# Scores of a head pair: two stacked 128-row products per head, or three 64-row products per head on the two halves of the array

## The reference

```python
qh = (q @ w_q).reshape(B, L, 16, 64).transpose(0, 2, 1, 3)
kh = (k @ w_k).reshape(B, L, 16, 64).transpose(0, 2, 1, 3)
vh = (v @ w_v).reshape(B, L, 16, 64).transpose(0, 2, 1, 3)
attn = einsum('bhqd,bhkd->bhqk', qh / 8, kh) + add_attn
attn = where(mask == 0, -1e9, attn);  attn = softmax(attn)
out = einsum('bhqk,bhkd->bhqd', attn, vh) @ w_o + residual;  out = layernorm(out)
```

## Time and profile before

| | |
|---|---|
| median of 3 runs | 3976.67 us (3975.65 to 3981.02) |
| the profiled execution | 3981.92 us |
| its span, first to last instruction | 3980.1 us |
| granted TensorE clock, mean | 0.99 |
| busy: PE, DVE, ACT, POOL | 95%, 68%, 56%, 46% |
| stages L0a and L0b | about the first 1440 us |

### The profile page before, as it was taken

The page is one execution under the profiler, slowest core; times in us unless marked ns, Lnnn a source line. Parts: engine busy times, 40 slices in busy tenths (PEclk is TensorE's granted clock), DMA queues, the critical chain, the costliest instruction groups (busy, mean ns, idle before and its releaser), DMA issues.

```text
span 3980.1 us, 63494 instructions
## 1 busy us (share of the span) xinstructions
PE 3767.7 (95%) x20700; PEld 2799.8 (70%) x20700; DVE 2724.9 (68%) x5801; ACT 2233.9 (56%) x4852; POOL 1847.6 (46%) x1905
## 2 busy tenths in 40 slices
PE   8999999999999998999999998999999979999999
PEld 6777677767777765666666766666666658888887
DVE  6666666677777777888888777888888853333334
ACT  6555555555555556777877767777777741111111
POOL 4444344344334345767767665666767631001001
PEclk9999999999999999999999999999999989999999
DMA  6666676554545466676666447776666671111000
GB/s 199 196 201 192 183 209 181 139 149 132 138 127 131 129 189 169 172 178 170 167 167 165 136 133 190 190 186 186 171 176 168 165 233 56 38 38 53 32 32 32
DMA packets 842517, 586.72 MB, mean 147 GB/s; under 512 B 611792, under 2 KB 660944, under 8 KB 841168
## 3 DMA queue, kind: packets, MB, share of 16 engines
q1 hardware_dynamic: 824400, 532.33, 50.0%
q10 hardware_dynamic: 17792, 50.33, 3.6%
HBM read 197.68 MB, written 238.55 MB: 110 GB/s over the span
## 4 chain that ended last, share of the span: by engine, by line
PE 40%; ACT 6%; DVE 6%; issue 5%; POOL 3%; DMA 3%; SPq 1%; DVEq 0%; POOLq 0%; ACTq 0%
PE psV L1529 5%; PE psT L1498 4%; PE psS L1477 3%; PE psJ L1422 3%; PE psS L1422 3%; PE psS L1424 3%; PE psS L1423 3%; PE psJ L1423 3%; PE psJ L1424 3%; POOL QS L2346 3%; PE psT L1422 2%; PE psT L1424 2%; PE psT L1423 2%; ACT PR L1805 2%; DVE PR L2001 1%
## 5 line engine op out<-in xcount | busy, mean ns | idle before, releaser
L2346 POOL TENSOR_SCALAR QS<-QK 32x1024 fp32r<-32x1024 f32 (+2 forms) x1152 | 1228.3, 1066 | 893.3 <-DVE QK L2015 434.9
L1805 ACT ACTIVATE PR<-PR,MN 128x512 f32<-128x512 f32 x1536 | 1101.5, 718 | 674.9 <-DVE MN L1997 518.1
L1997 DVE CUSTOM_DVE_ANT_0 PR<-psS,RAW 128x512 f32<-128x512 f32 x1024 | 694.2, 682 | 429.7 <-PE psS L1474 313.8
L1498 PE MATMUL psT<-ID,PR 128*128 128x128 f32 x3912 | 599.5, 276 | 95.8 <-ACT PR L1805 94.9
L1498 PEld LDWEIGHTS psT<-ID,PR 128*128 128x128 f32 x3912 | 475.8, 141 | 231.4 <-ACT PR L1805 142.3
L1529 PE MATMUL psV<-plain 128*32 128x512 f32 (+1 forms) x3072 | 510.3, 612 | 34.9 <-DMA plain<-split_rows 21.8
L1477 PE MATMUL psS<-QS 128*128 128x512 f32 x1024 | 456.8, 448 | 26.1 <-DVE PR L2001 14.0
L2001 DVE TENSOR_SCALAR_CACHE_REDUCE PR<-psS 128x512 f32<-128x512 f32 x512 | 345.3, 682 | 122.4 <-PE psS L1477 119.5
L1844 ACT ACTIVATE PR<-psS,COLS 128x512 f32<-128x512 f32 x128 | 88.3, 690 | 547.0 <-PE psS L1424 542.3
L2093 DVE COPY plain<-psT 128x512 f32<-128x512 f32 x530 | 361.2, 681 | 0.2 <-PE psT L1498 0.2
L2067 DVE CAST QK<-PR 128x512 fp32r<-128x512 f32 x128 | 59.2, 463 | 398.0 <-ACT PR L1844 352.6
(11 more groups left out here) (142 smaller groups left out, 8343.5 us busy)
## 6 DMA issues: line engine op xcount, KB each, us to landing
split_rows<-plain SPq DMA_DIRECT2D x366, 256.0 KB, 2.7
split_rows<-RAW SPq DMA_DIRECT2D x192, 256.0 KB, 2.5
x<-Y SPq DMA_DIRECT2D x96, 256.0 KB, 2.4
RAW<-x SPq DMA_DIRECT2D x96, 256.0 KB, 3.6
W<-kept ACTq DMA_DIRECT2D x12, 2048.0 KB, 11.3
Y<-x SPq DMA_DIRECT2D x96, 256.0 KB, 3.4
kept_c<-R SPq DMA_DIRECT2D x32, 512.0 KB, 3.9
kept<-ROWS SPq DMA_DIRECT2D x32, 512.0 KB, 3.6
```

Of the source, the lines that this page charges most:

```text
L1498: mm = nc.tensor.transpose(dst[:, kt * P:(kt + 1) * P], prob(st, k)[:, kt * P:(kt + 1) * P], ID[:, :])
L1805: nc.scalar.activation(prob(st, k), prob(st, k), ACT.Exp, bias=MN[:, k % 8:k % 8 + 1], scale=-1.0, accum_out=row_sums(st, SM, g)[:, qt, j: ...
L1997: nc.vector.tensor_tensor_reduce(out=prob(st, k), in0=psS[:, n % 2], in1=FB[:, k % NT], scale=-st.scale, scalar=BIG, op0=ALU.add, op1=ALU. ...
L2346: nc.gpsimd.tensor_scalar(to, pair, 1.0, 1.0, ALU.mult, ALU.mult).then_inc(stacked, 1)
```

## The change

In L0a and L0b the stacked copy goes. `score_pair` computes the same query tile of both heads of a group together: three matmuls for each head, with the 64 rows of that head as contraction, in turn for the first and second head, into the two banks of `psS`. The three are Q high by K high, Q high by K low and Q low by K high. Score tiles are numbered so that an even and the next odd one are the two heads of a group (`part`); the even step issues all six matmuls and the odd one none. The pair waits until both banks have been evacuated. `MAX` of the odd tile stands 0.75 slot before its old place, just behind that of the even one, and its `EXP` 0.25 slot earlier. POOL has no `STACK` step in these stages. `QS`, free now, takes Q and K of the odd groups, so that `J_HI` waits for scores of two groups earlier and no longer for the stacking. The stages of width 32 keep stacking.

```diff
 WIDE = {
-    "TILE": (1, 2, 3, 4),
-    "SENT": (1, 1.5, 2.5, 3.5),
+    "MAX": (0, -0.75),
+    "TILE": ((1, 0.75), (2, 2), (3, 3), (4, 4)),
+    "SENT": ((1, 1), (1.5, 1.5), (2.5, 2.5), (3.5, 3.5)),
...
-    "STACK": ((-1.5, -1, -1), (-5, -5, -5)),
...
+def part(st, k):
+    if st.dk == 32:
+        return divmod(k, NT)
+    group, n = divmod(k, 2 * NT)
+    return 2 * group + n % 2, n // 2
...
-        def qk(st, g):
-            return FB.bitcast(F32R) if bank(st, g) else QK
+        def qk(st, g, n):
+            if laid(st) and g % 2:
+                return QS[:, 1, n] if n < 3 else QS[:, 0, 2]
+            return QK[:, n]
...
+            def score_pair(st, k, b):
+                n = tal["s"].next()
+                if k % 2:
+                    return
+                g, qt = k // (2 * NT), part(st, k)[1]
...
+                pe.wait_ge(s_evac, tal["s"].done(n - 1))
+                tile = slice(qt * P, (qt + 1) * P)
+                for q, kk in ((0, 2), (0, 3), (1, 2)):
+                    for j in range(2):
+                        rows = slice(j * st.dk, (j + 1) * st.dk)
+                        mm = nc.tensor.matmul(psS[:, (n + j) % 2], qk(st, g, q)[rows, tile], qk(st, g, kk)[rows],
+                                              start=(q, kk) == (0, 2), stop=(q, kk) == (1, 2))
+                        if (q, kk) == (1, 2):
+                            mm.then_inc(s_full, 1)
...
-                if st.dk == 64:
-                    nc.tensor.matmul(psS[:, n % 2], q[:, tile], kk, start=True, stop=False)
-                    mm = nc.tensor.matmul(psS[:, n % 2], q[:, tile], k_lo, start=False, stop=True)
```

More of the change, by code:

```diff
@@ L227 @@
 SECOND = {
-    "TILE": (1, 2, 3, 4),
-    "SENT": (1, 2, 3, 5.6),
+    "MAX": (0, 0),
+    "TILE": ((1, 1), (2, 2), (3, 3), (4, 4)),
+    "SENT": ((1, 1), (2, 2), (3, 3), (5.6, 5.6)),
     "PV": (8, 8.5, 10, 10),
@@ L384, in timetable @@
         add(s, "SCORE", s)
-        add(s, "MAX", s)
+        add(s + table["MAX"][s % 2], "MAX", s)
         names = ("EXP", "SPLIT", "BOUNCE", "FETCH") if s in sent(st, b) else ("EXP", "TURN", "P_HI", "P_LO")
         for step, after in zip(names, table["SENT" if s in sent(st, b) else "TILE"]):
-            add(s + after, step, s)
+            add(s + after[s % 2], step, s)
     for h in range(NH):
@@ L398, in timetable @@
                 add(NT * h + (after[g] if isinstance(after, tuple) else after), step, g)
-        for piece in range(3):
+        for piece in range(3 if st.dk == 32 else 0):
             add(NT * h + table["STACK"][0 if h % st.per_group == 0 else 1][piece], "STACK", (h, piece))
@@ L1087, in count_turns @@
                 b = batch + off if at is None else at
-                if step == "EXP":
+                if step == "SCORE":
+                    score_at[st.name, b, k] = len(score_at) + 1
+                elif step == "EXP":
                     exp_at[st.name, b, k] = len(exp_at) + 1
@@ L1312, in fetch @@
                 sp.wait_ge(bounced[n % 4], times(n))
-                if last_product(st, b, k // NT):
-                    sp.wait_ge(pv_full, last_product(st, b, k // NT))
-                sp.dma_start_transpose(probs_of(ring(st, b, k // NT), k % NT).bitcast(U16),
+                h, qt = part(st, k)
+                if last_product(st, b, h):
+                    sp.wait_ge(pv_full, last_product(st, b, h))
+                sp.dma_start_transpose(probs_of(ring(st, b, h), qt).bitcast(U16),
                                        split_rows[n % 4].rearrange("q h k -> (q h) k")).then_inc(fetched[n % 4], 16)
@@ L1327, in run @@
                         if st.bias:
-                            tal["s"].mark(("side", k % NT))
+                            tal["s"].mark(("side", part(st, k)[1]))
                         if st.dk == 64:
@@ L1457, in x_turn @@
                 mm.then_inc(j_full, 1)
+            def score_pair(st, k, b):
[3 more added lines that the diff above has]
+                g, qt = k // (2 * NT), part(st, k)[1]
+                if qt == 0:
+                    split = max(tal["j"].marked(((kind, g), st.name, b)) for kind in "QK")
+                    pe.wait_ge(j_evac, tal["j"].done(split))
+                pe.wait_ge(s_evac, tal["s"].done(n - 1))
[7 more added lines that the diff above has]
+                            mm.then_inc(s_full, 1)
             def score(st, k, first):
@@ L1464, in score @@
                     if first and st.name == "SA" and h < 2:
-                        pe.wait_ge(qs_zero, 2 + h)
+                        pe.wait_ge(qs_zero, 1 + h)
                     i = tal["stack"].next()
@@ L1469, in score @@
                 tile = slice(qt * P, (qt + 1) * P)
-                q, kk, k_lo = (QS[:, h % 2, c] for c in range(3))
-                if st.dk == 64:
-                    nc.tensor.matmul(psS[:, n % 2], q[:, tile], kk, start=True, stop=False)
-                    mm = nc.tensor.matmul(psS[:, n % 2], q[:, tile], k_lo, start=False, stop=True)
-                else:
-                    mm = nc.tensor.matmul(psS[:, n % 2], q[:, tile], kk, start=True, stop=True)
-                mm.then_inc(s_full, 1)
+                q, kk = (QS[:, h % 2, c] for c in range(2))
+                nc.tensor.matmul(psS[:, n % 2], q[:, tile], kk, start=True, stop=True).then_inc(s_full, 1)
             held, gathered = {}, {}
@@ L1492, in turn @@
                 dst = turn_place(st, b, k)
-                at, head = ring(st, b, k // NT), (st.name, b, k // NT)
+                h = part(st, k)[0]
+                at, head = ring(st, b, h), (st.name, b, h)
                 if held.get(("head", at)) != head:
@@ L1631, in run @@
                     first = b == 0
-                    if step == "SCORE":
+                    if step == "SCORE" and laid(st):
+                        score_pair(st, k, b)
+                    elif step == "SCORE":
                         score(st, k, first)
@@ L1765, in context_hi, with projection_hi @@
                 nc.scalar.activation(cT[:, 0, kt], loaded("cs", buffer), ACT.Copy).then_inc(cs_hi, 1)
-            def projection_hi(st, name):
+            def projection_hi(st, name, b):
                 n = tal["j"].next()
@@ L1770, in projection_hi @@
                 kind, g = name[0], name[1]
-                if kind in "QK":
-                    used = tal["stack"].marked(("group", bank(st, g)))
+                if kind == "V":
+                    return
+                if laid(st):
+                    i, before = STAGES.index(st) * B + b, g - 2
+                    if before < 0:
+                        i, before = i - 1, before + NG
+                    if i >= 0:
+                        act.wait_ge(s_evac, 2 + score_at[STAGES[i // B].name, i % B, 2 * NT * (before + 1) - 1])
+                else:
+                    if st.name == "SA" and b == 0 and g == 0:
+                        act.wait_ge(s_evac, 2 + score_at["L0b", B - 1, 2 * NT * (NG - 1) - 1])
+                    used = tal["stack"].marked("group")
                     if used is not None:
                         act.wait_ge(stacked, tal["stack"].done(used))
[L1775 to L1778, removed]
                 act.wait_ge(j_full, tal["j"].done(n))
                 col = bias_col(st, kind, g)
-                nc.scalar.activation(qk(st, g)[:, 2 * "QK".index(kind)], psJ[:, n % 2], ACT.Identity,
+                nc.scalar.activation(qk(st, g, 2 * "QK".index(kind)), psJ[:, n % 2], ACT.Identity,
                                      bias=COLS[:, col:col + 1]).then_inc(j_hi, 1)
@@ L1802, in exponential @@
                 act.wait_ge(s_evac, tal["s"].done(n))
-                h, qt = divmod(k, NT)
+                h, qt = part(st, k)
                 g, j = divmod(h, st.per_group)
@@ L1850, in run @@
                         exponential(st, k)
-                        if st.name == "SA":
-                            tal["s"].mark("pairs")
                     elif step == "SPLIT" and split_by_act(st, k):
@@ L1878, in run @@
                     elif step == "J_HI":
-                        projection_hi(st, k)
+                        projection_hi(st, k, batch + off if at is None else at)
                     elif step == "OUT_SUM":
@@ L1895, in run @@
                         if k[0] % st.per_group == st.per_group - 1:
-                            tal["stack"].mark(("group", bank(st, k[0] // st.per_group)))
+                            tal["stack"].mark("group")
                     elif step == "RELU":
@@ L1991, in largest @@
                     dve.wait_ge(*split_at[before])
-                if (st.bias == "side" or first and st.bias) and k < NT:
-                    i = tal["side_ready"].marked(k)
+                h, qt = part(st, k)
+                if (st.bias == "side" or first and st.bias) and h == 0:
+                    i = tal["side_ready"].marked(qt)
                     dve.wait_ge(side_ready, tal["side_ready"].done(i))
@@ L1997, in largest @@
                     nc.vector.tensor_tensor_reduce(
```

(21 more changed lines are left out.)

5 lines of the change are left out of this document (1 added, 4 removed), and 35 rows, old and new, of the table SEAM.

## The result

The changed kernel takes 4010.0 us, median of 4 runs (4007.5 to 4012.7), against 3976.2 of the kernel before in the same session: the ratio is 1.0083 with a 95% interval of 1.0070 to 1.0095. It is slower by 34 us; 4008 was forecast. The profiled execution has a span of 4010.9 us against 3980.1, 30.8 more.

A forecast was written before the change was run, and what follows sets the result against it. PE's matmul stream, start to start, was taken as the bound. Per pair 0.687 + 0.41 − 0.916 = +0.181 us, × 256 = +46; −8 shared mode changes, −7 waits: +31 on 3976.7 gives 4008 us, range 3920 to 4050.

The forecast's parts named there:

- Products side by side: Score pairs on PE: the array's two row halves work at once, so six matmuls take 3 × 0.229 = 0.687 us.
- Rival 3: Score pairs: row halves do not work side by side; +117 us, with mode changes +214, so 4094 to 4190; chance 0.08.
- The change of mode: Around each pair on PE: standstill plus uncovered weight load, 0.09 + 0.11 going in, 0.10 + 0.11 out, 0.41 us.
- rivals 1 and 2: Mode change at pairs: 1, no standstill, 3928 us, chance 0.34; 2, standstill but loads covered, 3968 to 3985, chance 0.08.
- Of the bounds, 0.52: Upper bound in us for a pair's mode change, if the two halves' weight loads also come one after the other.
- Shared changes of mode: 36 of 256 pairs are followed at once by PV, one mode change serving both: −36 × 0.21 = −8 us.
- Waits: Scores on PE waiting for the maximum and stacking, 18.0 + 4.7 us: a third given back by slower PE, −7 us.
- moved steps: Odd maximum ahead of a copy and a projection's low part: PE jobs needing psJ may wait; 0, at most 13 us.
- The moved maximum: Odd tile's maximum on DVE needs the PR buffer of three tiles back; if it waits, copies behind it wait too.
- The pair's wait for both banks: Pair's wait on PE until both score banks are evacuated: covered by some 4 us, since the next pair comes 5.6 later.
- rival 4: Pairs wait for DVE's maximum: +97 us if every second pair waits, +50 for a quarter, 4058 us; chance 0.04.
- The give-back of rival 1: If mode changes are free, a 59 us saving in which longer waits on DVE and the score chain return 10 us.

The follow-up runs named there:

- kernel of four full matmuls: Changed kernel with its order, pairs and no stacking, but four 128-row matmuls for each pair instead of six of 64 rows, one product left out: 3986.5 us, ratio 1.0028.
- kernel of three full matmuls: Changed kernel with three 128-row matmuls for each pair instead of six of 64 rows, products left out: 3953.5 us, ratio 0.9944.
- joined `PV`: Kernel before with the two halves of a group's PV in one block at slot 8.75, nothing else: 3984.4 us, ratio 1.0015.

## Why the prediction was right

**Products side by side, 0.687 us: right.** The two of a couple start 3 to 4 ns apart, and a couple takes 0.235 us from first to first, so three take 0.705. The account has −58.1 us of steps where 0.229 × 256 = 59 was forecast; with 0.235 it is −55. Rival 3 is out. The Trainium skill (TensorE: Matmul & The Clock Gate, "Measured speedup vs the span model") counts about 4 ns of issue for each further tile that runs beside the first. The changed kernel's 3 to 4 ns agree; one head after the other it is 10 ns, which do not.

**The change of mode, 0.41 us: right, and it decides.** Borrowed from a change by columns on f32 operands, it holds for rows on fp32r: 0.09 in, 0.11 on the first couple's step (0.333 against 0.232), 0.09 out, 0.11 on the step behind. The doubt that the standstill came from f32 falls with it, as do rivals 1 and 2. A pair costs 1.100 us, 0.184 more than before against 0.181 forecast. Compared with its own counterpart in the kernel of four full matmuls, a pair that no `PV` touches takes some 0.16 us more behind transposes and 0.17 to 0.19 behind a matmul of 512 columns. Of the bounds, 0.52 is out: the two halves' loads start together. (Where the prediction calls 0.687 alone the second rival's number, it is the first's.)

**Shared changes of mode, −8: right within what can be told.** Steps and changes of mode sum to +37.0, where the terms of the prediction give 46 − 8 = 38.

**Waits, −7, and moved steps, 0: both off, and they nearly cancel.** The rest fell by 1.9 only, but the kernel of four full matmuls splits this: +9.9 for the new order and −11.8 for the slower PE. So a slower PE did give back the 7 forecast or more (some 5 of the 11.8 may be changes of mode that the account prices too high, see the 0.16 above), though not from the waits that were named: those for the maximum stayed at 18 us, and only stacking's 4.7 went. And the moved steps cost some 10 us and not 0, inside the bound of 13 and mostly where it was looked for, in projections that wait for DVE, though for the low part of `R` and not for the low parts of Q and K. Forecast −7 in all, −2 came. That 4008 fell within 2 us of 4010 is luck to this extent.

**The moved maximum: what it waits for was seen wrong.** I had it wait for the transposes of three tiles back. What it waits for is the reciprocals' turn, 31 times, because tiles 7 and 15 do not share the three buffers but the one beside them. That wait is 106 us of DVE's time and little of PE's: without 64 of them the time is 3 us shorter, inside the noise.

**The pair's wait for both banks: right.** The pair waits 18.8 us in 38 waits where single tiles waited 18.0 in 17, under the 40 that would have given rival 4 weight.

**The give-back of rival 1, 10 us: four times too small.** The kernel of three full matmuls has 61 us less of steps and changes of mode than the one before, and 22 us less time. That is a give-back of some 39 us, of which about 10 belong to the clock and not to waits. It touched only a rival, but it would have spoiled its number: with the mode free, about 3954 and not 3928.

## What to carry to other kernels

Fewer columns streamed is not less time when the matmuls need the array in another mode: count how many visits to that mode there are and price each with a standstill and an uncovered load on both sides; here three steps in place of four did not pay for one visit. By these prices (0.41 us for a visit, 0.23 for a step) a visit would have to save two steps to pay; that is an estimate, and no run had a longer block of such matmuls. In this case the price could be read from other visits in the same trace, though they parted the array by columns.

On an engine at 96% neither a saving nor a cost arrives whole. Of the 22 us that joined `PV` saved in the kernel before, 22 came back in the rest; of the 39 between the changed kernel and the one of four full matmuls, 12. Read the other way round, those 39 are a cost, of which 28 arrive. That the change as a whole shows +37 of work and +34 in time is two effects that offset each other: the reorder that came with it costs 10 us of its own. A change of order that rides along with a change of work wants a kernel of its own, with the old work in the new order; without it the 10 us look like part of the price of the mode. And before a missing saving is put down to waits, the time at the lower clock level is to be compared: in the kernel of three full matmuls it explains about 10 us of 41.

## What the hardware showed unexpectedly

Matmuls on the two row halves need not alternate in the program to run side by side: three for one half followed by three for the other take 0.91 us, as long as the six in turn (0.90). Weight loads for the two halves start together, 0.53 us for all six records, so the second half's load adds nothing. Where PE waited for nothing else, the standstill on a change of mode was 0.09 us whichever way the array was parted (32 columns, 64 columns, 64 rows) and in both directions.
